# Two attention stages: the key's transposes in another bank, the value products first in TensorE's step, the logarithm ahead of the key's eviction

## The reference

```python
ln_out = _ln(hidden_states, ln_w, ln_b)
q = _fp8_linear_pertensor(ln_out, wq, wq_scale, q_in_scale).reshape(b, s, g, hpg, d)
q = _ln(q, qln_w, qln_b)
k = _fp8_linear_pertensor(ln_out, wk, wk_scale, k_in_scale).reshape(b, s, g, d)
k = _ln(k, kln_w, kln_b)
v = _fp8_linear_pertensor(ln_out, wv, wv_scale, v_in_scale).reshape(b, s, g, d)
core = _gqa(q, k, v).reshape(b, s, nh * d)
...
kvx = jnp.einsum('bsi,oi->bso', cond, w_kv_x)
...
xout = _gqa(qx, kx, vx).reshape(b, s, nh * d)
cat = jnp.concatenate([core, xout], axis=-1)
catq = _div_clamp_fp8(cat, proj_smooth)
return jnp.einsum('bsi,oi->bso', catq, wproj) * (proj_in_scale * proj_w_scale)
```

## Time and profile before

| | |
|---|---|
| time, median of 3 runs | 1180.98 us (1179.11 to 1182.12) |
| profiled execution | 1176.74 us, its span from first to last instruction 1175.0 us |
| busy over the span | TensorE 77%, its weight loads 67%, VectorE 81%, ScalarE 60%, GpSimd 34% |
| 320 to 640 us (self attention) | TensorE 310.0, weight loads 269.9, VectorE 278.7, ScalarE 245.8, GpSimd 131.3 us busy; granted clock 1.00 |
| 680 to 1080 us (cross attention) | TensorE 383.5, weight loads 343.7, VectorE 325.3, ScalarE 276.2, GpSimd 143.5 us busy; granted clock 0.99 |

### The profile page before, as it was taken

How to read it: one execution, slowest core, us unless ns; L and a number is a source line. 1 busy time by engine, 2 the same in 40 slices (tenths; PEclk the granted TensorE clock), 3 DMA queues, 4 the chain that set the end, 5 groups by cost and what they waited for, 6 DMA issues and landing times. The chain is left out here.

```text
span 1175.0 us, 23858 instructions
## 1 busy us (share of the span) xinstructions
PE 903.1 (77%) x6878; PEld 781.6 (67%) x6878; DVE 946.7 (81%) x2442; ACT 710.1 (60%) x2471; POOL 394.0 (34%) x498
## 2 busy tenths in 40 slices
PE   3610067423999999999999469999999999998638
PEld 3510033212888888888888358888888888887627
DVE  7989989887888888888888558888888888886461
ACT  3454044374877777777778457667667677674303
POOL 0009900000344444444443443333333433333124
PEclk9965588756999999999999779999999999999559
DMA  6022100002000000000000120000000000000400
GB/s 218 1 108 71 36 1 0 0 0 108 2 1 1 0 0 0 0 0 0 0 0 0 41 86 6 6 7 7 4 4 4 9 4 4 0 0 1 148 19 18
DMA packets 18267, 26.96 MB, mean 23 GB/s; under 512 B 1265, under 2 KB 15409, under 8 KB 17457
## 3 DMA queue, kind: packets, MB, share of 16 engines
q1 hardware_dynamic: 17840, 25.41, 6.3%
q0 software_dynamic: 384, 1.05, 0.3%
HBM read 23.83 MB, written 2.62 MB: 23 GB/s over the span
## 5 line engine op out<-in xcount | busy, mean ns | idle before, releaser
L1392 ACT ACTIVATE c_p<-c_kT_sc_ps,c_nmax 128x64 f32<-128x64 f32 x256 | 76.7, 312 | 72.4 <-DVE c_nmax L1257 72.4
L1213 POOL TENSOR_TENSOR c_cat<-c_tb,c_mb 128x512 fp32r<-128x512 bf16 x64 | 74.4, 1162 | 137.5 <-DVE c_tb L1291 137.5
L1213 POOL TENSOR_TENSOR s_cat<-s_tb,s_mb 128x512 fp32r<-128x512 bf16 x64 | 74.3, 1161 | 116.4 <-DVE s_tb L1291 116.4
L1392 ACT ACTIVATE s_p<-s_kT_sc_ps,s_nmax 128x64 f32<-128x64 f32 x256 | 76.8, 312 | 48.5 <-DVE s_nmax L1257 48.5
L1409 PE MATMUL s_qo_ps<-wq,s_xqf 128*128 128x512 f32 x256 | 71.8, 403 | 32.4 <-POOL s_xqf L1195 32.4
L1409 PE MATMUL c_qo_ps<-wq,c_xqf 128*128 128x512 f32 x256 | 72.1, 404 | 16.4 <-DVE wv L645 16.4
L1473 PE MATMUL c_pj_ps<-wp,c_cat 128*128 128x256 f32 x512 | 78.0, 296 | 1.5 <-POOL c_cat L1213 1.5
L1473 PE MATMUL s_pj_ps<-wp,s_cat 128*128 128x256 f32 x512 | 77.4, 295 | 2.2 <-POOL s_cat L1213 2.2
L1339 DVE TENSOR_TENSOR c_yb<-c_qo_ps,c_ism 128x512 bf16<-128x512 f32 x64 | 44.3, 692 | 43.0 <-PE c_qo_ps L1444 43.0
L1218 POOL TENSOR_TENSOR c_pn<-c_p,c_rsum 128x256 f32<-128x256 f32 x64 | 39.3, 614 | 118.1 <-DVE c_rsum L1346 118.1
L1218 POOL TENSOR_TENSOR s_pn<-s_p,s_rsum 128x256 f32<-128x256 f32 x64 | 39.3, 614 | 106.4 <-DVE s_rsum L1346 106.4
(11 more groups left out here) (359 smaller groups left out, 2889.0 us busy)
## 6 DMA issues: line engine op xcount, KB each, us to landing
x_res<-in_x SPq DMA_DIRECT2D x4, 512.0 KB, 5.8
vT<-in_ctxT SPq DMA_DIRECT2D x2, 1024.0 KB, 10.5
tf_work<-in_wqT SPq DMA_DIRECT2D x2, 1024.0 KB, 6.0
tf_work<-in_wprojT SPq DMA_DIRECT2D x2, 1024.0 KB, 5.5
w_work<-in_wqxT SPq DMA_DIRECT2D x2, 1024.0 KB, 6.5
w_work<-in_wkvxT SPq DMA_DIRECT2D x2, 1024.0 KB, 8.0
c_ctx<-in_ctxT SPq DMA_DIRECT2D x16, 128.0 KB, 2.3
w_work<-in_wprojT SPq DMA_DIRECT2D x2, 1024.0 KB, 5.7
```

Source lines behind the costliest of these rows:

```text
L1213: nc.gpsimd.tensor_tensor(cat[out8.o % 2][:], tb[:], mb[:], ALU.subtract).then_inc(cat_ready, 1)
L1392: nc.scalar.activation(pe_s[:, a * S:(a + 1) * S], sc_ps[:, a * S:(a + 1) * S], ACT.Exp, bias=nmax[:, a:a + 1], accum_out=psum_s[:, a:a + ...
```

## The change

Four things, in both stages:

1. The key's transposes go into the unused half of bank 1 of `qo_ps`, and the scores get a bank of their own. The transposes wait for `yb` of two units before instead of for the exponentials; the scores take over the wait for the exponentials; the transposes of the probabilities, which write the same bank 1, wait for the key's eviction.
2. TensorE's step begins with the value products (before: after the key and value products), and the key's transposes stand behind the output projection instead of ahead of it.
3. ScalarE: the logarithm and the exponential stand ahead of the key's eviction, and the query's square ahead of the eviction of the probabilities.
4. VectorE: the third step of the rounding stands between the first two Newton steps, the fourth behind `qn`.

```diff
--- before.py
+++ after.py
@@ -1125,8 +1125,7 @@
         kv_ps = [psum(f"kv_ps{i}", [P, 2 * KW]) for i in range(2)]
         qT_ps = psum("qT_ps", [P, QW])
 
-        kT_sc_ps = psum("kT_sc_ps", [P, 512])
-        kT_ps, sc_ps = kT_sc_ps[:, 0:KW], kT_sc_ps[:, KW:KW + 4 * S]
+        kT_ps, sc_ps = qo_ps[:, 1, GU * P:GU * P + KW], psum("sc_ps", [P, 512])[:, 0:4 * S]
         pj_ps = psum("pj_ps", [P, 512])
 
         prep = k["dve_chain"]
@@ -1309,7 +1308,7 @@
                     if u.live:
                         norm_guess()
                     if f8.live:
-                        for part in range(3):
+                        for part in range(2):
                             round8(part)
                     if pj.live and pj.o % UT == UT - 1:
 
@@ -1322,12 +1321,15 @@
                             nc.vector.bn_stats(k["stat6"][:, bass.ds(tile_of(i, o, 4), 1), :].rearrange(
                                 "p a c -> p (a c)"), xt)
                     if u.live:
-                        for part in range(3):
-                            newton(part)
+                        newton(0)
+                    if f8.live:
+                        round8(2)
+                    if u.live:
+                        newton(1)
+                        newton(2)
+                        normalised_query()
                     if f8.live:
                         round8(3)
-                    if u.live:
-                        normalised_query()
                     if sm.live:
                         maxima()
                     if u.live:
@@ -1366,24 +1368,25 @@
                         act.wait_ge(tq_done, sm.count(1, 1))
                         nc.scalar.activation(qT[:], qT_ps[:], ACT.Identity, scale=lnp[:, 0:1], bias=lnp[:, 1:2]
                                              ).then_inc(qT_ready, 1)
-                        act.wait_ge(t_done, sm.count(1, 1))
-                        nc.scalar.activation(kT[:], kT_ps, ACT.Identity, scale=col(f"k{pre}ln_w"),
-                                             bias=col(f"k{pre}ln_b")).then_inc(kT_ready, 1)
                     if u.live:
                         chain.at(u.count(1))
                         act.wait_ge(var_ready, u.count(1, 1))
                         chain(nc.scalar.activation(l6[:], v6[:], ACT.Ln))
                         wait_unit(act, r_ready, u.before(1))
                         nc.scalar.activation(g6[:], l6[:], ACT.Exp, scale=-0.5).then_inc(rs_ready, 1)
+                    if sm.live:
+                        act.wait_ge(t_done, sm.count(1, 1))
+                        nc.scalar.activation(kT[:], kT_ps, ACT.Identity, scale=col(f"k{pre}ln_w"),
+                                             bias=col(f"k{pre}ln_b")).then_inc(kT_ready, 1)
+                    if q.live:
+                        act.wait_ge(q_done, q.count(1, 1))
+                        wait_unit(act, var_ready, q.before(1))
+                        nc.scalar.activation(sq[:, 0:QW], q_bank(q), ACT.Square).then_inc(sqq_ready, 1)
                     if pv.live:
                         act.wait_ge(pt_done, pv.count(1, 1))
                         nc.scalar.activation(pT[:], po_ps[:, 0:GU * P], ACT.Copy).then_inc(pT_ready, 1)
                     if own_kv and q.live and o in CrossHead.WITH_UNITS:
                         cross_head_act(act, nc, aw, work, chunks, i, o)
-                    if q.live:
-                        act.wait_ge(q_done, q.count(1, 1))
-                        wait_unit(act, var_ready, q.before(1))
-                        nc.scalar.activation(sq[:, 0:QW], q_bank(q), ACT.Square).then_inc(sqq_ready, 1)
                     if sm.live:
                         act.wait_ge(max_ready, sm.count(1, 1))
                         wait_unit(act, pn_ready, sm.before(1))
@@ -1413,6 +1416,16 @@
 
                 def step(i, o):
                     u, kv_u, t, pt, pv, pj = units(i, o, 0, 1, 2, 3, 4, 5)
+                    if pv.live:
+                        pe.wait_ge(pT_ready, pv.count(1, 1))
+                        pe.wait_ge(qn_ready, min(pv.n + 3, UNITS) if pv.static else pv.count(1, 3))
+                        for g in range(GU):
+                            for b in range(2):
+                                rows = slice(b * S, (b + 1) * S)
+                                last = nc.tensor.matmul(out_banks(pv)[:, b, g * P:(g + 1) * P],
+                                                        v_s[pv.o % 4][rows, g * D:(g + 1) * D],
+                                                        pT[rows, g * P:(g + 1) * P], start=True, stop=True)
+                        last.then_inc(pv_done, 1)
                     if kv_u.live:
                         gp, tp = kv_u.o % UT, (kv_u.o // UT) % 2
                         wait_unit(pe, kn_ready, kv_u.before(2))
@@ -1435,16 +1448,6 @@
                                                                 stop=(n == 3 * KC - 1))
                                         n += 1
                         last.then_inc(kv_done, 1)
-                    if pv.live:
-                        pe.wait_ge(pT_ready, pv.count(1, 1))
-                        pe.wait_ge(qn_ready, min(pv.n + 3, UNITS) if pv.static else pv.count(1, 3))
-                        for g in range(GU):
-                            for b in range(2):
-                                rows = slice(b * S, (b + 1) * S)
-                                last = nc.tensor.matmul(out_banks(pv)[:, b, g * P:(g + 1) * P],
-                                                        v_s[pv.o % 4][rows, g * D:(g + 1) * D],
-                                                        pT[rows, g * P:(g + 1) * P], start=True, stop=True)
-                        last.then_inc(pv_done, 1)
                     if t.live:
                         pe.wait_ge(qn_ready, t.count(1, 1))
                         wait_unit(pe, qT_ready, t.before(1))
@@ -1454,12 +1457,6 @@
                             qcols = qT_ps[:].rearrange("p (g b h s) -> p g b h s", g=GU, b=2, h=HPG)[:, g, :, h, :]
                             last = nc.tensor.transpose(qcols, qn[:, a * P:(a + 1) * P], ident[:])
                         last.then_inc(tq_done, 1)
-                        pe.wait_ge(kn_ready, t.count(1, 1))
-                        wait_unit(pe, kT_ready, t.before(1))
-                        wait_unit(pe, exp_ready, t.before(1, 4))
-                        for a in range(GU):
-                            last = nc.tensor.transpose(kT_ps[:, a * P:(a + 1) * P], kn[:, a * P:(a + 1) * P], ident[:])
-                        last.then_inc(t_done, 1)
                     if pj.live:
                         gpj = pj.o % UT
                         if not own_kv and pj.static and pj.n == 0:
@@ -1475,6 +1472,13 @@
                                                         start=(gpj == 0 and a == 0 and part == 0),
                                                         stop=(gpj == UT - 1 and a == HU - 1 and part == 1))
                         last.then_inc(pj_done, 1)
+                    if t.live:
+                        pe.wait_ge(kn_ready, t.count(1, 1))
+                        wait_unit(pe, kT_ready, t.before(1))
+                        wait_unit(pe, y_ready, t.before(2))
+                        for a in range(GU):
+                            last = nc.tensor.transpose(kT_ps[:, a * P:(a + 1) * P], kn[:, a * P:(a + 1) * P], ident[:])
+                        last.then_inc(t_done, 1)
                     if u.live:
                         gp, tp = u.o % UT, (u.o // UT) % 2
                         if gp == 0:
@@ -1486,12 +1490,14 @@
                     if pt.live:
                         pe.wait_ge(pn_ready, pt.count(1, 1))
                         wait_unit(pe, y_ready, pt.before(1))
+                        pe.wait_ge(kT_ready, min(pt.n + 2, UNITS) if pt.static else pt.count(1, 2))
                         for g in range(GU):
                             last = nc.tensor.transpose(po_ps[:, g * P:(g + 1) * P], pn[:, g * P:(g + 1) * P], ident[:])
                         last.then_inc(pt_done, 1)
                     if t.live:
                         pe.wait_ge(qT_ready, t.count(1, 1))
                         pe.wait_ge(kT_ready, t.count(1, 1))
+                        wait_unit(pe, exp_ready, t.before(1, 4))
                         for g in range(GU):
                             for b in range(2):
                                 a = g * 2 + b
```

## The result

The changed kernel took 1230.17 us (median of 4 runs, 1228.19 to 1232.97) against 1180.51 us for the kernel before. The ratio is 1.0422, with a 95% interval of 1.0396 to 1.0448. The forecast was 1201, in a range of 1187 to 1220: the sign was right, the size was 49.7 us instead of 20.

What follows compares the result with a forecast made beforehand. It took order as the bound: a loop through late key, value products, projections and square. Self adds nothing, cross goes from 6.05 to 6.37 us, 0.32 x 64 = 20 us, so 1201 against 1181.0; range 1187 to 1220.

Steps and rivals of the forecast that it cites:

- The loop: Reduction through late key, value products, projections and square to next reduction: 5.72 us in self, 6.19 in cross; chance 0.62.
- the waits that it named: TensorE for the key's eviction, VectorE's reduction for the key's square, and in fourth units the value products for `qn`.
- those that it said would go: TensorE's wait before the key's transposes, 0.22 us a unit in cross, and VectorE's for the value products.
- The key loop: Same chain from reduction to reduction; in cross 3.32 + 0.65 + 1.60 + 0.12 + 0.50 = 6.19 us.
- 0.17 + 0.89: TensorE's slots behind the late key: 0.17 us for the probabilities' two transposes, then 0.89 for the scores.
- rival of longer loops: Transposes at 0.21, 0.1 more at semaphores, GpSimd's conversions on the variance: 0.2 us a unit, 1227 us; chance 0.08.
- The fourth unit: Each fourth unit, where output is added into `x_res` ahead of the Newton steps: 6.90 us in cross, 5.91 in self.
- Self attention: Quiet unit from 5.69 to 5.72 us, fourth one slightly shorter; nothing gained or lost over 64 units.
- The query loop alone: Rival: key ready earlier, so the loop through `qn` decides, 5.65 us in self, 6.25 in cross: about 1187; chance 0.13.
- The guard of the bank: Probabilities' transposes wait for the key's eviction in the shared bank; guarding by address would make the key loop 0.17 shorter.

Runs made afterwards that it cites:

- run 1: Changed kernel with the value products put back behind the key and value projections in TensorE's step: 1221.44 us, ratio 1.0351.
- run 2: Changed kernel with ScalarE's old order, key's eviction ahead of the logarithm and that of the probabilities ahead of the query's square: 1218.73 us, ratio 1.0319.
- run 5: Kernel before with the change's bank and VectorE's order only; product order and logarithm's place as before: 1170.92 us, ratio 0.9907.
- run 3: Kernel before with only the value products moved first in TensorE's step: 1236.33 us, ratio 1.0472.
- run 6: Kernel before with ScalarE's order alone, logarithm ahead of the key's eviction and query's square ahead of that of the probabilities: 1201.47 us, ratio 1.0177.
- run 12: Kernel before with only the logarithm and the exponential ahead of the key's eviction, query's square left in place: 1202.64 us, ratio 1.0171.
- run 4: Changed kernel with GpSimd's conversions and head means cut to 4 columns after the first round, other data stale: 1215.16 us, ratio 1.0293.
- run 9: Changed kernel with the x_res addition and its statistics moved from ahead of the Newton steps to behind the normalised key: 1224.47 us, ratio 1.0361.
- run 8: Kernel before with VectorE's order of the change alone: 1171.11 us, ratio 0.9927.
- run 7: Kernel before with the key's transposes in the other bank, and the waits this brings, alone: 1174.32 us, ratio 0.9941.
- run 11: Kernel before with VectorE's order, the bank, and the x_res addition and statistics moved behind the normalised key: 1163.45 us, ratio 0.984.

## Why the prediction was right in sign and wrong in size

**The loop: right.** The prediction took the change for a question of order and summed the loop reduction, logarithm, key, scores, value products, projections, square. That is the loop of the trace after, with the waits that it named, and without those that it said would go. Runs 1, 2 and 5 show that the product order and the logarithm's place are the causes. Each alone also costs (run 3: 55 us, about 8 of them the clock's; runs 6 and 12: 21 us), but through a loop of its own: the query's in run 3, the one through `yb` in runs 6 and 12.

**The key loop's terms: too small by 0.17 in a quiet cross unit** (6.19 forecast, 6.36 measured). From the transposes' load to the value products I took 0.17 + 0.89; it is 0.27 + 1.04, 0.25 more. The 0.27 lies outside even the bounds that I gave, 0.17 to 0.21; what makes it longer is not shown. The 0.89 was read where projections follow the scores. The loads of the projections overlap the end of the scores' loads, those of the value products do not: 905.14 + 0.97 = 906.11, next load 906.18. The key's eviction gives 0.05 back, the value products 0.01 and the way from the square to the reduction 0.02. In self the scores take 1.04 too (490.84 to 491.88), and the units without a stretched step take 5.85 to 5.88 where I had 5.72. Run 4 has these terms without the stretched steps: its periods are 0.09 (self) and 0.14 us (cross) above the forecast ones of 5.77 and 6.37, some 15 us in all.

**GpSimd: left out of the sum.** The prediction named the conversions on the variance in its rival of longer loops and priced all of that rival at 0.2 us a unit; the sum has nothing for it. Run 4 prices the stretched steps alone: 15 us. In self attention I had not seen that the head means would move onto the variance too. Before, the long one began 1.02 us after the reduction and just behind the variance step (480.20 against 480.17), now it begins 0.97 after it and just ahead (489.12 against 489.13). Likely this is because the reciprocal, which they follow, no longer waits behind `yb` for the value products; no run tests it.

**The fourth unit: right**, 6.90 forecast and 6.91 measured, with `qn` as the wait that was named; run 9 confirms it. **Self attention: wrong**, "nothing" against 17 us (period 5.99 against 5.72). Most of it is the two items above. Another 3 us stood in the forecast's own figures: it gave a period of 5.77 against 5.72 and added nothing for it.

The step that failed is thus the sum of the key loop. Its order was right and its sizes were too low: a group's slot was taken from a place with another neighbour (0.89, measured 1.04), the transposes were taken at 0.17 (measured 0.27), and the variance step was taken as it was, at nothing extra, where it measured 0.74 us in one cross unit of four and about 0.4 in most self units. Of the 32 us that the two stages grew beyond the 20 forecast, about 15 are the slots, 14 the stretched steps (by the periods of run 4) and 3 the fraction dropped in self.

**The query loop alone as the fallback: incomplete.** The prediction took what is left without the key loop to be the query's loop (1187). Run 1 showed a third one, through `yb` in VectorE's queue, which the prediction has nowhere; it is the loop of run 6 too, 21 us above the kernel before. The rival's sum also has a slip: 5.72 - 5.65 is 0.07 us a unit and not 0.1, which gives 1189 instead of 1187 as the lower end. This had no part in the miss.

**The guard of the bank: not free, but paid for.** Where the key is early, the shared bank's wait holds TensorE's weight loads for 0.23 us in each cross unit (run 5). The bank also ends the wait for the exponentials, which without it (run 8) was 10.0 us over 53 units, 0.19 a unit on average. The two about cancel, which is why the bank, worth 6 us alone (run 7), is worth nothing beside VectorE's order (run 5 against run 8). Where the key is late, the transposes stand behind it, which may be the 0.15 us a unit between runs 1 and 6.

What stays open: why the transposes' slot is 0.27 us, how much GpSimd's stretched steps cost the kernel before, why the bank gains 6 us alone although it brings its wait there too, and why it costs 3.6 us in run 11.

## What to carry to other kernels

In a pipeline over several engines, price a step that moves on one queue by the loops that it closes: write each unit's chain from its first instruction to the same one of the next unit, through every in-order queue, and take the longest, since undoing one cause can leave an equal loop (runs 1, 2 and 5). Look at each instruction that stands ahead of the chain's start in a queue, even if its own data isn't the chain's. Take a group's slot from a row with the same neighbour. And when a releaser moves, follow where GpSimd's operations will land, since a small VectorE step beside them can take several times as long (run 4).

## What the runs showed of the hardware

The first weight load of 64 rows for the value products began only after the scores' loads ahead were done (0.07 after, at 906.18), where a load of 128 rows began 0.08 before that end (482.03 against 481.14 + 0.97). A VectorE step of six columns took 0.74 us instead of 0.17 when a GpSimd operation of 0.74 us began 0.02 us ahead of it. And in run 3, after TensorE had sat idle for 1.55 us, six loads of 128 rows took 1.35 us (from 915.45, granted clock 0.51 from 916 to 918) instead of 0.77.
